# One number in a beat table: where the second half of the next batch's x is loaded and split (attention and routed FFN, one core)

## What is computed

```python
qkv = x @ W_attn + b_attn                      # 512 -> 3 * 512
q, k, v = heads(qkv)                           # 16 heads of 32
scores = k . q / sqrt(32), causal mask, softmax over the keys
x = layernorm(x + (attn @ v) @ W_out + b_out)
scores = x @ w_router
top_scores, top_idx = top_k(scores, 512)       # of the 1024 tokens of a batch
h = gelu(x[top_idx] @ W1 + b1)                 # 512 -> 2048
update = sigmoid(top_scores) * (h @ W2 + b2)
out = layernorm(x + scatter_add(x, top_idx, update))
```

## Time and profile before

| | us |
|---|---|
| median of 3 runs | 2569.15 (2568.43 to 2572.22) |
| the profiled execution | 2572.62 |
| its span, first to last instruction | 2570.9 |
| PE busy | 2485.0 (97%) |
| DVE busy | 1667.6 (65%) |
| POOL busy | 1595.2 (62%) |
| ACT busy | 1190.1 (46%) |
| mean granted TensorE clock | 0.977 |

### The profile page before, as it was taken

How to read it: one execution, slowest core, us unless ns; L and a number is a source line. 1 busy time by engine, 2 the same in 40 slices (tenths; PEclk the granted TensorE clock), 3 DMA queues, 4 the chain that set the end, 5 groups by cost and what they waited for, 6 DMA issues and landing times. The chain is left out here.

```text
span 2570.9 us, 40263 instructions
## 1 busy us (share of the span) xinstructions
PE 2485.0 (97%) x13920; PEld 1831.9 (71%) x13920; DVE 1667.6 (65%) x4231; ACT 1190.1 (46%) x2034; POOL 1595.2 (62%) x1666
## 2 busy tenths in 40 slices
PE   7999999999999999999999999997999999999998
PEld 5565676677676676776776767763688888888886
DVE  5667677677777777776777777677555535543533
ACT  2555566566665656655665666555431111111110
POOL 1677788887888788888878888886132113131211
PEclk8999999999999999999999999997999999999999
DMA  7656668677677766767766686762430101010000
GB/s 143 93 99 132 116 153 175 126 166 146 133 149 129 181 137 124 177 127 145 160 151 132 133 173 140 149 157 89 146 99 25 34 25 42 19 39 25 21 30 17
DMA packets 167260, 286.43 MB, mean 111 GB/s; under 512 B 23121, under 2 KB 58001, under 8 KB 165906
## 3 DMA queue, kind: packets, MB, share of 16 engines
q1 hardware_dynamic: 159890, 267.01, 48.7%
q0 software_dynamic: 7168, 16.85, 2.1%
HBM read 116.97 MB, written 65.11 MB: 71 GB/s over the span
## 5 line engine op out<-in xcount | busy, mean ns | idle before, releaser
L796 POOL TENSOR_TENSOR Pa<-Pa,Pm 128x512 f32<-128x512 f32 (+1 forms) x623 | 770.7, 1259 | 117.1 <-ACT Pm L919 100.6
L1409 PE MATMUL PS<-Qp,Kp 98*128 98x512 f32 (+3 forms) x1536 | 496.8, 359 | 24.9 <-ACT Pm L919 12.5
L1377 PE MATMUL PS<-Kp,Qp 96*128 96x512 f32 (+3 forms) x1536 | 496.6, 361 | 15.7 <-DVE nm L1018 6.1
L919 ACT ACTIVATE Pm<-PS 128x512 f32<-128x512 f32 (+1 forms) x643 | 357.7, 567 | 289.4 <-PE PS L1409 247.5
L1018 DVE TENSOR_REDUCE nm<-PS 128x1 f32<-128x512 f32 x512 | 344.8, 687 | 182.4 <-PE PS L1377 182.2
L796 POOL TENSOR_TENSOR Pa<-Pa,P 128x512 f32<-128x512 f32 (+1 forms) x307 | 382.2, 1267 | 56.1 <-ACT P L919 47.7
L1377 PEld LDWEIGHTS PS<-Kp,Qp 96*128 96x128 f32 x1536 | 285.0, 195 | 118.6 <-issue 44.5
L1409 PEld LDWEIGHTS PS<-Qp,Kp 98*128 98x128 f32 x1536 | 282.8, 193 | 106.7 <-ACT Pa L919 28.5
L1026 DVE CUSTOM_DVE_ANT_0 PS<-PS,maskA 128x384 f32<-128x384 f32 (+3 forms) x512 | 245.8, 509 | 160.4 <-PE PS L1377 160.0
L886 ACT ACTIVATE G<-PS,b1c 128x512 f32<-128x512 f32 x128 | 88.2, 689 | 539.6 <-PE PS L1461 520.6
L1026 DVE CUSTOM_DVE_ANT_0 PS<-PS,maskA,nm 128x384 f32<-128x384 f32 (+3 forms) x512 | 267.0, 554 | 91.4 <-PE PS L1377 85.9
(11 more groups left out here) (142 smaller groups left out, 4223.2 us busy)
## 6 DMA issues: line engine op xcount, KB each, us to landing
Qp<-nat SPq DMA_DIRECT2D x192, 256.0 KB, 7.4
Kp<-nat SPq DMA_DIRECT2D x192, 256.0 KB, 6.2
o_s<-Of SPq DMA_DIRECT2D x64, 256.0 KB, 2.3
Ot<-o_s SPq DMA_DIRECT2D x64, 256.0 KB, 3.1
xb<-in_x SPq DMA_DIRECT2D x64, 256.0 KB, 3.2
h_s<-hs SPq DMA_DIRECT2D x64, 256.0 KB, 2.5
out<-xb SPq DMA_DIRECT2D x64, 256.0 KB, 2.5
x_raw<-in_xt SPq DMA_DIRECT2D x15, 1024.0 KB, 6.7
```

Of the source, the lines that this page charges most:

```text
L796: e.tensor_tensor(to, to, probs(u, k)[:, h0:h0 + many, 0:w], ALU.add).then_inc(s["padd"], many)
L919: e.activation(probs(u, k)[:, hh[0]:hh[-1] + 1, 0:w], PS[:, B_BANKS[j % 2], 0:len(hh) * w].rearrange("p (h n) -> p h n", n=w), ACT.Exp).th ...
L1377: ins = e.matmul(to, Qp[0:96, u % 4, h_, qt * P:qt * P + P], Kp[0:96, (2 * i + k0 // 512) % 4, h_, 0:w], start=True, stop=True)
L1409: ins = e.matmul(PS[:, B_BANKS[j % 2], x_ * w:x_ * w + w], Kp[0:98, (2 * i + k // 4) % 4, h_, k % 4 * P:k % 4 * P + P], Qp[0:98, u % 4, h_ ...
```

## The change

One number of the beat table: the second half of x of batches 1 to 7 now stands at beat -25 instead of -21. The first half (-30) and all of batch 0 stay.

```diff
-        load_x = {BEATS * 8 * b - (21 if c else 30): (b, c) for b in range(1, B) for c in range(2)}
+        load_x = {BEATS * 8 * b - (25 if c else 30): (b, c) for b in range(1, B) for c in range(2)}
```

## The result

| us | before | after |
|---|---|---|
| median | 2570.14 (6 runs, 2567.66 to 2572.42) | 2580.78 (6 runs, 2579.37 to 2582.50) |
| the profiled execution | 2572.62 | 2579.86 |
| its span | 2570.9 | 2578.1 |

The ratio is 1.0044 (95%: 1.0034 to 1.0054): the change makes the kernel 10.6 us, or 0.44%, slower. That is inside the range, but 6.8 us above the forecast; it is the time of rival 3. The two profiled executions lie only 7.2 us apart, because the one of before is slower than all its timed runs and the one of after is near the fastest of its own.

What follows compares the result with a forecast made beforehand. PE's one real attention stall per batch waits for ACT, whose queue waits for POOL's L812. Terms 2.4 (delay), 0.8 (batch 7), 1.8 (clock) and -0.2 (batch 1) sum to +4.8 us: 2574.0 us, range 2566 to 2583.

Steps and rivals of the forecast that it cites:

- rival 3: DVE and clock: low parts hold up N job or layer norm, five or six falls; 2580 to 2585 us, chance 0.18.
- The load's issue and landing: On SP: the load of x is still held by PE and lands 5.5 us after issue; it gains nothing.
- gaps: On PE: new stalls of about 1.8 us before tile (3,1) and 1.0 before (3,2), 2.8 in all.
- The old stall: On PE before tile (4,3), 1.80 us ahead of batch 3: it would be gone.
- The low parts on DVE: On DVE, moved ahead of L1082: costed at nothing, with only 0.4 us of cover for the Q job.
- the clock: PE's half rate after stalls, three falls in six batches kept, 1.45 us each instead of 0.88: +1.8 us.
- the delay: PE's lateness from tile (4,3) to the sums, partly absorbed: 0.4 us per batch, +2.4 us over six.
- batch 1: Ahead of batch 1: tile (3,2) slips 2.1 us, waits of some 2.3 us vanish; -0.2 us, give or take 2.
- Batch 7 and the end: Ahead of batch 7: its load took 6.3 us and ACT now waits for it, +0.8 us.
- rival 1: Whole kernel: a small loss, the forecast itself, 2571 to 2577 us; chance 0.45.
- rival 2: ACT's wait is absorbed up to the sums and nothing changes, 2567 to 2571 us; chance 0.27.

Runs made afterwards that it cites:

- The filled kernel: Ten discarded matmuls put into PE's two gaps ahead of batches 2 to 7, against the changed kernel; 2575.11 us, ratio 1.0021 to the kernel before.
- -26: Second half of x at beat -26 instead of -21, against the kernel before; 2588.39 us, ratio 1.0070.
- -25 with the later norm: The change with ACT's L974 and L976 one beat later, against the kernel before; 2578.34 us, ratio 1.0033.
- -24: Second half of x at beat -24 instead of -21, against the kernel before; 2574.47 us, ratio 1.0007.
- the norm later at -21 and -22: ACT's L974 and L976 one beat later, x at beat -21 or -22, against the kernel before; 2564.05 us (0.9978) and 2570.97 us (1.0000).
- -22: Second half of x at beat -22 instead of -21, against the kernel before; 2572.73 us, ratio 1.0003.
- the last experiment: Fourth low part on DVE one beat sooner, on top of x at -21 with L974 and L976 one beat later; 2574.07 us, ratio 1.0014 to the kernel before.

## Why the prediction was right and where it fell short

*What held.* The load's issue and landing (5.5 us, 6.1 to 6.3 in batches 7 and 1) did not change. ACT waited 1.88 us for 1.85. Tile (3,2) ran 8.55 us after the issue against 5.88 before, 2.67 later for 2.8, in gaps of 1.54 and 0.70 for 1.8 and 1.0. L812 ended 14.7 us behind the issue (654.22 + 0.27 - 639.78), as worked out (652.9 - 638.35 = 14.55). The old stall was gone. Tile (4,3) came 18.74 us after the issue against 16.26, 2.48 later; 4.41 - 2.72 = 1.69 of that is the half rate from the sums to the K job, and the 0.8 left is the forecast's.

*What cost nothing, as said, at beat -25.* The low parts on DVE. Their row for the whole program has a median of 692 ns now, where the earlier trace rows had 1102. Two of the four ahead of batch 3 ran at 652.36 and 654.89, between two of POOL's stretches of additions, and took 0.65 and 0.68 us; the one at 649.52, beside them, took 1.72:

```profile
L1115 DVE TENSOR_TENSOR xTl<-x_raw,xTh x64: 646/692/1800, 5.3 to 1529.5; 128x512 fp32r<-128x512 f32 x64
```

*The step that failed: the clock.* "I take them as equal and keep three falls in six." The new gaps add up to more than the old one and were followed by a fall each time. Per batch, from batch 2 on, the text had 0.4 for the delay and 4.4 / 6 - 2.6 / 6 = 0.3 for the clock, 0.7 in all; measured were 1.0. The filled kernel takes the two apart: its four undisturbed batches have 217.26, against 216.80 for the one batch of before without a fall or another stall, so the delay is 0.46 for the forecast's 0.4; the change's 218.51 is 1.25 above, the price of one fall (forecast 1.45); and before already paid 217.50 - 216.80 = 0.70. 0.46 + 1.25 - 0.70 = 1.01. Not all of that 0.70 is the clock: three of the five batches had a fall and took 217.67, and a fourth, without one, took 217.70 with a wait of 0.67 us for DVE's maxima at 851.3. The price of a fall was right and the number of them was not, and for that number the text had no more reason than that it took the gaps as equal. What decides whether the clock falls behind a stall stays open. Rival 3 was half right, in its time and in its clock; that its low parts were not the cause was shown. That the median lies inside the range is owed to the range's reach into rival 3; the sum of the forecast had neither the six falls nor the loss in batch 1 that follows.

*The term that was missed: batch 1.* Forecast -0.2, measured +2.1. Its own steps held: tile (3,2) ran 9.38 us after the load for the forecast's 9.41, the 1.65 us wait for `xTl` was gone with waits of 0.94 for `Of` and 1.00 for `Pa` in its place, and 46 us after the load the kernel was 0.45 ahead. But around 290 us, half a batch on, the granted clock falls in both kernels after a stall that both have, and stays down longer in the changed one, 10.2 us for 6.8. Windows that begin with the sums of the N job, before and after:

```profile
290.60:294.00 3.40, 3.35 (x16) 0.59 (x16) 0.13 (x1) 1.16 (x2) 0.59 (x2) 0.50 1.08 127
294.00:297.40 3.40, 3.40 (x23) 2.94 (x20) 2.24 (x13) 0.98 (x2) 0.23 (x1) 0.92 0.61 138
```

```profile
288.70:292.10 3.40, 3.38 (x16) 0.59 (x16) 0.00 (x0) 1.16 (x2) 0.55 (x1) 0.50 1.09 126
292.10:295.50 3.40, 3.40 (x15) 2.93 (x12) 1.10 (x8) 0.49 (x1) 0.00 (x0) 0.50 0.60 136
```

Measured from the load, the changed kernel goes from 0.45 ahead to 2.0 behind in that piece. The kernels in which ACT waits over 3.4 us for the landing ahead of batch 1 and PE stalls for 1.0 us or more behind it (the change, the late V loads, the filled gaps, -26, ACT's copies alone at the new place, and -25 with the later norm) took 217.8 to 220.7 from this load to the mark of batch 2; all others took at most 217.3, also those at -24, with a wait of 3.17 and a stall of 0.50, and with the split load, 1.63 and 0.99 and a stall of 0.90. So it goes with the change and with PE's stall; by which link that reaches a stretch 90 us later was not tested and stays open.

*Batch 7 and the end* were forecast at 0.8 for the late landing and 0.7 for the batch, and have 1.6. ACT waited 2.47 us there, 0.6 more than elsewhere.

Sum: 2.1 + 5.0 + 1.6 = 8.7 for the forecast's 4.8.

*A slip in the chances.* Half of rival 1 and all of rival 3 are 0.405, and the other half with rival 2 is 0.495; the text has 0.43 and 0.47 and speaks of something left open, though its four chances add up to 1.

## What to carry to other kernels

Before moving a consumer of a DMA forward, look at what holds the issue of that DMA: if it stays where it is, the move only spends the cover, and on an in-order engine everything queued behind the wait pays as well. If the consumer has to stand early, let it wait for the part it reads (two loads with a semaphore each brought the whole 0.44% back), and look for the real owner of a stall before moving its neighbour: here it was the layer norm in ACT's queue, and moving that one alone gave 0.22%. A stall of PE has two prices, its length and the half rate behind it; count the falls of the clock in the profile of each variant, and look at the mean clock of its timed runs too, before reading anything into a difference of a few microseconds.

## What the runs showed of the hardware

The half rate is paid behind some stalls and not behind others. These are counts from one profiled execution of each kernel, ahead of batches 2 to 7. No fall followed where no stall of PE was longer than 1.32 us and none was followed within two matmuls by a second (-24 ahead of batches 2 to 6, and the norm later at -21 and -22). After a single stall of 1.65 to 1.80 it fell in three batches of six (before and -22), after one of 1.67 in five of six (the last experiment), after one of 2.24 in six of six. After a stall of 1.3 to 2.1 and one of 0.3 to 0.7 two matmuls behind it, it fell in six of six with the change and with -25 and the later norm, but in five with the V loads later and in four with only ACT's copies at the new place. At beat -26 (2.2 to 2.5 and 0.5) three of the six falls lasted 6.8 us instead of 3.4. So the length of a stall alone does not say whether the clock falls. Matmuls whose results nobody reads, put into a stall, kept the clock up and made the kernel faster than the change.

A load of 1 MB by SP took 5.3 to 5.6 us from issue to landing ahead of batches 2 to 6, with other loads issued right behind it or not, and 5.8 to 6.7 ahead of batches 1 and 7. Cut into two of 0.5 MB, ahead of batches 2 to 7, the first landed after 4.1 to 4.3 us and the second 5.4 to 5.9 us after the first issue, so the cut cost at most some 0.4 us at the end and gave 1.3 us at the front.

Where a low part of DVE (L1115) met additions of POOL (L796), it took up to 1.8 us for 0.68, or an addition took up to 1.8 us for 1.3.
